# Cross attention with its scores turned: tokens on the partitions, and the maxima turned and spread by TensorE

## The reference, cut to what matters

```python
kvx = jnp.einsum('bsi,oi->bso', cond, w_kv_x)
kx, vx = jnp.split(kvx, 2, axis=-1)
kx = _ln(kx.reshape(b, sc, g, d), kxln_w, kxln_b)      # keys, normalised per group
vx = vx.reshape(b, sc, g, d)
scores = jnp.einsum('bsghd,btgd->bghst', qx, kx) * scale   # 128 query rows x 1601 tokens
p = jax.nn.softmax(scores, axis=-1)                        # over the tokens
xout = jnp.einsum('bghst,btgd->bsghd', p, vx)
```

## Time and profile before

| | |
|---|---|
| runs | 2944.86, 2946.58, 2947.46 us; median 2946.58 |
| profiled execution | 2949.31 us, span 2947.5 us |
| busy in the span: PE, DVE, ACT, POOL | 2710.0 (92%), 1787.8 (61%), 1501.6 (51%), 465.9 us (16%) |
| mean granted TensorE clock | 0.960 of 2.4 GHz |
| TensorE busy, 400 to 1800 us | 192.7 to 193.7 us of each 200 |

### The profile page before, as it was taken

The page is one execution under the profiler, slowest core; times in us unless marked ns, Lnnn a source line. Parts: engine busy times, 40 slices in busy tenths (PEclk is TensorE's granted clock), DMA queues, the critical chain, the costliest instruction groups (busy, mean ns, idle before and its releaser), DMA issues.

```text
span 2947.5 us, 38368 instructions
## 1 busy us (share of the span) xinstructions
PE 2710.0 (92%) x13446; PEld 2196.7 (75%) x13446; DVE 1787.8 (61%) x4701; ACT 1501.6 (51%) x2892; POOL 465.9 (16%) x376
## 2 busy tenths in 40 slices
PE   6879999999999999999999999979998889878999
PEld 5767678677777787787786786758876778756887
DVE  6746536437337347356365365568768776557997
ACT  6934435325325335245244354436675567846776
POOL 4401102002002002011011020005332222012111
PEclk9978999999999999999999999999999999988999
DMA  3435002002011011020020021325666542429996
GB/s 118 129 85 176 18 19 84 4 23 80 2 45 58 3 59 43 4 72 29 5 84 18 17 74 40 128 99 157 177 178 173 136 100 59 174 72 384 374 373 238
DMA packets 247007, 303.09 MB, mean 103 GB/s; under 512 B 144024, under 2 KB 165144, under 8 KB 233504
## 3 DMA queue, kind: packets, MB, share of 16 engines
q1 hardware_dynamic: 244016, 296.36, 31.5%
q0 software_dynamic: 2800, 4.27, 0.6%
HBM read 259.48 MB, written 46.98 MB: 104 GB/s over the span
## 4 chain that ended last, share of the span: by engine, by line
PE 72%; DVE 13%; ACT 7%; DMA 3%; issue 3%; SPq 2%; POOL 1%; POOLq 0%; DVEq 0%; ACTq 0%
PE ps L103 18%; PE ps L105 17%; PE ps L104 17%; PE ps L729 5%; PE ps L746 3%; PE ps L711 3%; PE ps L776 2%; DVE lnw L824 1%; DVE lnw L1936 1%; DVE zz L1939 1%; ACT pr L950 1%; DVE cv L1903 1%; PE ps L767 1%; DMA ca<-cat_d 1%; ACT gb L1686 1%
## 5 line engine op out<-in xcount | busy, mean ns | idle before, releaser
L1062 POOL TENSOR_TENSOR lnw<-lnw,half 128x8 f32<-128x8 f32 (+1 forms) x104 | 170.8, 1642 | 1466.0 <-DVE lnw L829 1466.0
L103 PE MATMUL ps<-cnh,pth 128*128 128x512 f32 (+1 forms) x832 | 335.0, 403 | 13.7 <-ACT kn L950 13.7
L103 PE MATMUL ps<-whf,cth 128*128 128x512 f32 (+1 forms) x832 | 338.7, 407 | 7.0 <-DVE ctl L537 3.6
L105 PE MATMUL ps<-whf,ctl 128*128 128x512 f32 (+1 forms) x832 | 329.6, 396 | 0.0
L104 PE MATMUL ps<-wlf,cth 128*128 128x512 f32 (+1 forms) x832 | 329.2, 396 | 0.0
L105 PE MATMUL ps<-cnh,ptl 128*128 128x512 f32 (+1 forms) x832 | 328.8, 395 | 0.0
L104 PE MATMUL ps<-cnl,pth 128*128 128x512 f32 (+1 forms) x832 | 328.4, 395 | 0.0
L950 ACT ACTIVATE pr<-ps,lnw 128x128 f32<-128x128 f32 (+1 forms) x384 | 144.4, 456 | 162.3 <-DVE lnw L848 162.3
L981 ACT ACTIVATE pr<-ps,sm 128x1601 f32<-128x1601 f32 x64 | 102.5, 1602 | 243.0 <-DVE sm L868 215.9
L940 DVE TENSOR_SCALAR pc<-ps,sm 128x512 f32<-128x512 f32 x64 | 48.1, 751 | 289.3 <-PE ps L105 289.3
L2376 DVE TENSOR_TENSOR ml<-mr,mh 128x2048 fp32r<-128x2048 f32 x90 | 203.4, 2287 | 32.4 <-ACT mh L2320 32.4
(11 more groups left out here) (328 smaller groups left out, 6100.9 us busy)
## 6 DMA issues: line engine op xcount, KB each, us to landing
mr<-in_moe SPq DMA_DIRECT2D x90, 1024.0 KB, 7.1
ctr<-in_ctxt SPq DMA_DIRECT2D x96, 256.0 KB, 2.9
pr<-in_ctxn SPq DMA_DIRECT2D x96, 256.0 KB
wr<-in_wqkv SPq DMA_DIRECT2D x64, 256.0 KB, 2.9
wvf<-in_wattn SPq DMA_DIRECT2D x12, 1024.0 KB, 4.8
ca<-cat_d SPq DMA_DIRECT2D x16, 512.0 KB, 4.1
qk_d<-cv SPq DMA_DIRECT2D x32, 256.0 KB, 3.2
wr<-in_wz SPq DMA_DIRECT2D x32, 256.0 KB, 3.4
```

Source lines behind the costliest of these rows:

```text
L103: pe.matmul(dst, lh, rh, start=first, stop=False)
L105: return pe.matmul(dst, ll, rh, start=False, stop=last)
L1062: po.tensor_tensor(rs[0:w, s, :], nv[0:w, s, :], half[0:w, 0:8], ALU.pow).then_inc(kx_rs, 1)
```

## The change

Scores are made the other way round: for each tile of tokens the keys are the stationary operand and the query rows the moving one, so the result has tokens on the partitions, 13 blocks of 128 x 128 side by side in banks 0 to 3. The probabilities then need no transposes. Instead:

- VectorE takes, for each partition and query row, the maximum over the 13 blocks (`col_max_dv`): one strided reduction over twelve blocks, and one maximum with the 65 rows of the last.
- TensorE transposes that 128 x 128 (`max_turn_pe`); VectorE takes the maximum along it (`row_max_dv`), one per query row, and multiplies the identity by it (`dg`); TensorE multiplies a matrix of ones by that (`max_spread_pe`), so every partition has all 128 maxima.
- VectorE copies them and subtracts them in four pieces into SBUF (`p_sub_dv`), ScalarE takes the exponential in four pieces in place (`p_exp_ac`) and writes the high halves (`p_high_ac`), VectorE the low halves, now both out of SBUF.
- The sum: VectorE adds over the 13 blocks with a strided reduction over 1664 columns of `es` (`p_sum_dv`), TensorE multiplies that by a column of ones (`row_sum_pe`), VectorE takes the reciprocal (`rinv_dv`).

The turning, spreading and summing products, the `pc` transposes and the output product of the head before stand inside the PV loop, after the PV products of tile 3 and of tile 5 (of tile 8 and tile 10 in head 0). They use bank 4, PV uses bank 5. On VectorE the scaling of PV's result (`pc_dv`) stands between the low halves of the next head. Semaphores of earlier stages are used again with a base (`Again`); the counts of later stages are adapted. The context rows' buffer `cnr` and the probabilities no longer share memory.

```diff
+        def score_pe(pe, b, g, tiles):
+            m = 8 * b + g
+            for i in tiles:
+                o, w = TILES[i]
+                if g == 0:
...
+                    pe.wait_ge(k_out, 2 * (13 * b + i) + 2)
+                elif i % 4 == 0:
+                    pe.wait_ge(*p_sub.at(4 * (m - 1) + i // 4 + 1))
+                f = pe.matmul(ps[0:w, o:o + 128], kf[:, g, o:o + w], qb[:, g, :], start=True, stop=True)
+                if i >= 11:
+                    f.then_inc(scored, 1)
+        def max_turn_pe(pe, m):
+            pe.wait_ge(col_max, m + 1)
+            pe.transpose(turn_ps, cm[:, :], ident).then_inc(max_turned, 1)
+        def max_spread_pe(pe, m):
+            pe.wait_ge(*row_max.at(m + 1))
+            if m > 0:
+                pe.wait_ge(*p_sub.at(4 * m))
+            pe.matmul(spread_ps, one[:, :], dg[:, :], start=True, stop=True).then_inc(max_spread.sem, 1)
+        def row_sum_pe(pe, m):
+            pe.wait_ge(*p_summed.at(m + 1))
+            if m > 0:
+                pe.wait_ge(pc_out, m)
+            pe.matmul(sum_ps, cs_[:, :], one[:, 0:1], start=True, stop=True).then_inc(row_summed.sem, 1)
         def pv_pe(pe, b, g):
             m = 8 * b + g
             if m > 0:
                 pe.wait_ge(pc_out, m)
...
+            early, late = (3, 5) if g > 0 else (8, 10)
             for i in range(13):
...
                 if i % 4 == 0:
                     pe.wait_ge(p_low, 4 * m + i // 4 + 1)
-                f = three(pe, bank(6), pth[0:w, i, :], ptl[0:w, i, :], cnh[0:w, i, :], cnl[0:w, i, :], i == 0, i == 12)
+                f = three(pe, bank(5), pth[0:w, i, :], ptl[0:w, i, :], cnh[0:w, i, :], cnl[0:w, i, :], i == 0, i == 12)
+                if i == 12:
+                    f.then_inc(pv_done, 1)
+                elif i % 4 == 3:
+                    f.then_inc(p_used.sem, 1)
+                if i == early:
+                    row_sum_pe(pe, m)
+                    if g + 1 < 8:
+                        max_turn_pe(pe, m + 1)
...
+                    if g > 0:
+                        pc_turn_pe(pe, m - 1)
+                if i == late:
+                    if g + 1 < 8:
+                        max_spread_pe(pe, m + 1)
+                    if g > 0:
+                        xo_pe(pe, m - 1)
         def s3_pe(pe):
...
+                score_pe(pe, b, 0, (12,))
                 if b + 1 < NB:
+                    kx_pe(pe, 13 * b + 13, (0,), (2, 3))
+                max_turn_pe(pe, 8 * b)
+                if b + 1 < NB:
+                    kx_pe(pe, 13 * b + 13, (1,), (0, 1))
+                max_spread_pe(pe, 8 * b)
+                if b + 1 < NB:
+                    kx_pe(pe, 13 * b + 13, (1,), (2, 3))
                 for g in range(8):
                     if g + 1 < 8:
+                        score_pe(pe, b, g + 1, range(13))
                     pv_pe(pe, b, g)
+        def col_max_dv(dv, m):
+            dv.wait_ge(scored, 2 * m + 1)
+            t = vs(dv.tensor_reduce(cm[:, :], ps[:, 0:1536].rearrange("p (i q) -> p q i", i=12), AX.X, ALU.max))
+            dv.wait_ge(scored, 2 * m + 2)
+            dv.wait_ge(dv_step, t)
+            dv.tensor_tensor(cm[0:65, :], cm[0:65, :], ps[0:65, 1536:1664], ALU.max).then_inc(col_max, 1)
+        def row_max_dv(dv, m):
+            s = m % 2
+            dv.wait_ge(max_turned, m + 1)
+            t = vs(dv.tensor_reduce(mx[:, s:s + 1], turn_ps, AX.X, ALU.max))
+            t_rinv = rinv_dv(dv, m - 1) if m % 8 else None
+            dv.wait_ge(dv_step, t)
+            dv.tensor_scalar(dg[:, :], ident, mx[:, s:s + 1], None, ALU.mult).then_inc(row_max.sem, 1)
+            return t_rinv
+        def p_sub_dv(dv, m):
+            dv.wait_ge(*max_spread.at(m + 1))
+            t = vs(dv.tensor_copy(cm[:, :], spread_ps))
...
+            for p in range(4):
...
+                dv.tensor_tensor(piece(es, p, n), piece(ps, p, n), cm[0:n, :].unsqueeze(1).to_broadcast([n, q, 128]),
+                                 ALU.subtract).then_inc(p_sub.sem, 1)
+        def p_sum_dv(dv, m):
+            dv.wait_ge(p_exp, 4 * m + 4)
+            dv.tensor_reduce(cs_[:, :], es[:, :].rearrange("p (i q) -> p q i", i=13), AX.X, ALU.add).then_inc(p_summed.sem, 1)
         def s3_dv(dv):
...
+                col_max_dv(dv, 8 * b)
                 split_ctxn_dv(dv, 13 * b + 12)
+                row_max_dv(dv, 8 * b)
+                p_sub_dv(dv, 8 * b)
+                p_low_dv(dv, 8 * b, range(4))
+                p_sum_dv(dv, 8 * b)
                 for g in range(8):
                     m = 8 * b + g
+                    if g + 1 < 8:
+                        col_max_dv(dv, m + 1)
+                        t_rinv = row_max_dv(dv, m + 1)
+                        if g == 0 and b + 1 < NB:
+                            kx_stats_dv(dv, 13 * b + 13)
+                        p_sub_dv(dv, m + 1)
                     if g == 0 and b + 1 < NB:
                         kx_norm_dv(dv, 13 * b + 13)
+                    if g == 7:
+                        t_rinv = rinv_dv(dv, m)
                     if b == 7:
                         quantize_cat_dv(dv, g)
...
+                    if g + 1 < 8:
+                        p_low_dv(dv, m + 1, range(2))
+                        p_sum_dv(dv, m + 1)
+                        p_low_dv(dv, m + 1, (2,))
+                    pc_dv(dv, m, t_rinv)
+                    if g + 1 < 8:
+                        p_low_dv(dv, m + 1, (3,))
+        def p_exp_ac(ac, m, p):
+            n = 65 if p == 3 else 128
+            ac.wait_ge(*p_sub.at(4 * m + p + 1))
+            ac.activation(piece(es, p, n), piece(es, p, n), ACT.Exp, scale=SCALE).then_inc(p_exp, 1)
         def s3_ac(ac):
...
+                if b + 1 < NB:
+                    kx_norm_ac(ac, 13 * b + 13)
                 for g in range(8):
                     m = 8 * b + g
                     if g > 0:
                         pcT_ac(ac, m - 1)
+                    if g + 1 < 8:
+                        p_exp_ac(ac, m + 1, 0)
+                    if g > 0:
+                        xo_ac(ac, m - 1)
+                    if g + 1 < 8:
+                        p_exp_ac(ac, m + 1, 1)
+                        p_high_ac(ac, m + 1, 0)
+                        p_exp_ac(ac, m + 1, 2)
+                        p_exp_ac(ac, m + 1, 3)
+                        p_high_ac(ac, m + 1, 1)
                     if b == 7:
                         scale_cat_ac(ac, g)
...
+                    if g + 1 < 8:
+                        p_high_ac(ac, m + 1, 2)
+                        p_high_ac(ac, m + 1, 3)
```

More of the change, by code:

```diff
@@ L667, in s3_sp, with kx_pe @@
                         xo_store(sp, b, g - 1)
[L669 removed]
+        def kx_pe(pe, n, parts=(0, 1), chunks=(0, 1, 2, 3)):
             b, i = divmod(n, 13)
             w, s = TILES[i][1], n % 2
[L672 removed]
+            if parts[0] == 0 and chunks[0] == 0:
                 pe.wait_ge(ct_low, n + 1)
@@ L690, in kx_pe @@
             for part in parts:
-                for c in range(4):
+                for c in chunks:
                     f = three(pe, bank(KSET[i] + part)[0:w, :], cth[:, s, c, 0:w], ctl[:, s, c, 0:w],
                               wkh[:, c, 512 * part:512 * part + 512], wkl[:, c, 512 * part:512 * part + 512], c == 0, c == 3)
-            if parts[-1] == 1:
+            if parts[-1] == 1 and chunks[-1] == 3:
                 f.then_inc(kx_done, 1)
@@ L733, in p_turn_pe @@
-        def p_turn_pe(pe, b, g, parts):
-            m, s = 8 * b + g, g % 2
-            for w in parts:
-                if w == 0:
-                    pe.wait_ge(p_exp, m + 1)
-                if w >= 2:
-                    pe.wait_ge(p_low, 4 * m + w - 1)
-                elif g > 0:
-                    pe.wait_ge(p_low, 4 * (m - 1) + w + 3)
-                else:
-                    pe.wait_ge(k_out, 2 * (13 * b + 12) + w + 1)
-                for i in range(4 * w, min(4 * w + 4, 13)):
-                    o, n = TILES[i]
-                    f = pe.transpose(bank(4 + w % 2)[0:n, 128 * (i % 4):128 * (i % 4) + 128], pr[:, s, o:o + n], ident)
-                f.then_inc(p_turned, 1)
+                    if i == 0:
+                        pe.wait_ge(d_qb, 16 * (b + 1))
+                        pe.wait_ge(kn_ac, 13 * b + 11)
+                        pe.wait_ge(kn_dv, 13 * b + 11)
+                    elif i == 8:
+                        pe.wait_ge(kn_ac, 13 * b + 12)
+                        pe.wait_ge(kn_dv, 13 * b + 12)
@@ new lines, in p_sum_dv, with rinv_dv, p_low_dv @@
+        def p_sum_dv(dv, m):
+            dv.wait_ge(p_exp, 4 * m + 4)
+            dv.tensor_reduce(cs_[:, :], es[:, :].rearrange("p (i q) -> p q i", i=13), AX.X, ALU.add).then_inc(p_summed.sem, 1)
+        def rinv_dv(dv, m):
+            dv.wait_ge(*row_summed.at(m + 1))
+            return vs(dv.reciprocal(rinv[:, m % 2:m % 2 + 1], sum_ps))
+        def p_low_dv(dv, m, parts):
+            for p in parts:
+                n = 65 if p == 3 else 128
+                q = min(4, 13 - 4 * p)
```

(11 more changed lines are left out.)

176 lines of the change are left out of this document (55 added, 121 removed).

## The result

The changed kernel took 3076.84 us in the median of four runs (3075.49 to 3080.66), beside 2945.72 (2942.69 to 2947.46) for the kernel before on the same chip: a ratio of 1.044, 95% interval 1.0427 to 1.0454. Slower, as forecast (3066, range 2980 to 3150); 11 us of the 131 that it lost were not in the forecast. The profiled execution has a span of 3074.2 us against 2947.5.

What follows compares the result with a forecast made beforehand. TensorE was taken as the bound, busy for all 14.39 us of a later head. The profiled 2949.3 us plus 63 for seven batches and 54 for batch 7 gave 3066 us, range 2980 to 3150.

Steps and rivals of the forecast that it cites:

- TensorE's share: TensorE's work in a later head: 13.56 us instead of 14.39, a gain of 0.83 where TensorE sets the pace.
- VectorE's prices: VectorE's two strided reductions at 1.7 ns a value: column maximum 2.75 us, column sum 2.97.
- The chain of an ordinary head: From S, the start of a head's PV, through VectorE, TensorE and ScalarE to the scaling: next PV at S + 14.7.
- Head 1: Batches 0 to 6: PV waits behind key statistics and ScalarE's key normalisation; TensorE idles 8 us after its scores.
- Batch 7: Quantisation of the concatenated heads stands in the chain: heads 19.8 us against 14.39; 43 us late, 54 with the clock.
- The clock: After TensorE's long gaps the granted clock falls to 0.50: 1.7 us in each head 1, 11 in batch 7.
- last head 14.0 to its end against 12.9: Last head of each of batches 0 to 6, to the next batch's start: 1.1 us later than before.
- heads 0 and 1: Batches 0 to 6: head 0 ends 3.9 us earlier, but both together end 6.4 late per batch.
- Strides free: Rival: both VectorE reductions at 1.06 ns a value, ordinary heads gain 0.83 each; 2992 us, chance 0.2.
- The clock holds: Rival: TensorE keeps 2.4 GHz in the gaps, 1.7 x 7 and 11 us less; 3043 us, chance 0.07.
- TensorE stays the bound: Rival: VectorE reaches the scaling before TensorE ends the next scores in every head; 2872 us, faster given chance 0.08.
- the rival's two conditions: For TensorE to stay the bound, batch 7 would have to lose 4.9 us and head 1 its 8 us queue.

Runs made afterwards that it cites:

- contiguous sum: Changed kernel with VectorE's column sum reading its 13 values next to each other instead of 512 bytes apart (row sums wrong): 2998.7 us, ratio 1.0175.
- early scaling: Changed kernel with VectorE scaling the PV result before the next head's column sum instead of after it: 3018.64 us, ratio 1.0246.
- moved sum: Changed kernel with, from head 1 on, the column sum behind the next head's column maximum, scaling before the last two low halves: 2982.36 us, ratio 1.012.
- products in the gaps: Changed kernel with unread TensorE products ahead of PV in head 1, the last head and batch 7: 3046.38 us, ratio 1.0337.
- the best order of the same work: Kernel with all moves, plus later spread, head 2's maximum ahead of key normalising (ScalarE alone), head 0's result turned one head later: 2906.02 us, ratio 0.9861.

## Why the prediction was nearly right

**TensorE's share** held. Without waits a later head takes 13.69 (contiguous sum) against the 13.56 worked out.

**VectorE's prices.** The column sum was right (2.97 forecast, 3.03 measured). The column maximum was mis-sized: 2.75 forecast, 1.75 measured, because I gave PSUM the surcharge that the earlier trace rows show; those rows read SBUF (`cv`). (L1936 of the kernel before does not read runs of w neighbours: it reads entries that lie 128 bytes apart, each of them w times. For single values, w = 1, that makes no difference.) The error hardly reached the time, since TensorE comes to the turn only after twelve products and the row sum, S + 3.0; the maximum with its tail is done at 1248.33, S + 2.2, and VectorE then waits 1.15 for the turn. At the forecast price it would have been ready at about S + 3.2: some 0.2 a head.

The Trainium skill (Advanced Engine Details and Errata, Memory Cachelines) gives SBUF lines of 16 bytes, of which each wants at least two hits, and PSUM lines of 8 bytes, where, with matmuls in view, it asks that every two consecutive elements be contiguous. The sum out of SBUF agrees (3034 against 1878 ns); the maximum out of PSUM, where single strided values cost VectorE nothing, does not follow the second, and the measurement decides. The Trainium skill (VectorE: DVE Perf Modes, Mode 1x), by which odd strides work in the mode of one result a cycle, fits the maximum and not the sum.

**The chain of an ordinary head** held step by step: turn, spread, first subtraction and second high half at S + 3.0, 5.0, 6.5 and 9.6 (forecast 3.3, 5.2, 6.75, 9.85), period 14.65 (14.7); of the 0.25 won by the second high half 0.2 go again in the last part, 5.05 instead of 4.85. The early scaling and the moved sum show that it is a chain of places and not of VectorE's total.

**Head 1** held: 7.45 us of idling (8), head 0's PV done 1218.10 - 1.18 - 1197.85 = 19.1 behind the key product, against 23.4 in the earlier trace rows, so 4.3 early (3.9), PV 1 at 30.9 behind the key product at 1197.85 (31.5 by the forecast's sum). The two causes that it named are the ones that the experiments take away: ScalarE's queue is worth 2.6 of it, the place of the scaling 3.5.

**Batch 7** held in its mechanism, and its price without the clock is what the products in the gaps show: 19.6 to 20.1 against the 19.8 worked out.

**The clock** was sized well where the forecast put a fall: head 1 1.97 (16.60 - 14.63) for 1.7, batch 7 10.2 (167.91 - 157.70) for 11, together 24 us for 23. What failed is the step "last head 14.0 to its end against 12.9": it has no clock in it, though the last head's PV waits 3.5 us and the clock is at 0.50 for 3 to 7 us around its start in each of the seven batches. By TensorE's rows, from the end of head 6's PV to the next key product, it takes 15.65 in batch 4 (1319.19 - 3.50 to 1331.34), 15.6 to 16.9 in the seven and 16.3 in the mean. That is 2.3 a batch over the forecast, 16 us in seven, and 14 of them came back when the gap was filled (14.3).

**That the total came so near** is in part luck, a balance of errors. Between the two profiled executions the loss was 126.7 and the forecast 117, 9.7 short. Too low were the last heads, by 16, and batch 7, by 5.6 (59.6 for 54; more than half of it in its last head, 23.7 from the end of head 6's PV for the 19.1 and 1.6 of the forecast). Too high by 6.6 were heads 0 and 1, in the mean 5.5 late for 6.4: the forecast took head 0 of batch 4 of the kernel before, 23.4, for all seven, but in four of them the clock falls among the key tiles and it takes 24.0 to 24.9. The ordinary heads (1.4 for 1.5), the key tiles and the stages behind, which had no term, gave back 5.5.

**The rivals' prices.** Each condition could be made. Strides free, 2992: 2998.7 with the contiguous sum (the maximum was free already). The clock holds, 3043: 3046.4 with the gaps filled, though with 30 us back and not 23, since the last heads are in it. TensorE stays the bound, 2872: the best order of the same work came to 2906. What is left lies in head 1 (15.08 for 13.56) and batch 7 (114.64, still above 108.31), as the rival's two conditions said, and also in head 2 (14.79) and the ordinary heads behind it (13.8).

## What to carry to other kernels

An engine at 70% can set the end through the order of its instructions alone: follow one loop from a wait back to itself through all engines, and put long operations that nobody waits for (here the sum) where that engine itself waits. Where a wait goes when one link moves tells a loop from a queue. To each gap of a few us that a change opens on TensorE add the clock that is lost behind it, in every place where it opens, and not only in the largest.
